# A hand-ordered attention and mixture-of-experts kernel: four scores for maxima, the routing steps and one projection change their places

## The chip, the core and the metric

One core of a Trainium2 chip runs the whole kernel. The metric is device time in microseconds (us). TensorE multiplies matrices into PSUM, VectorE, ScalarE and GpSimd work on vectors, SyncE issues transfers (DMA). Each engine runs its own list of instructions in order and waits at semaphores for the others.

## What is computed

Eight sequences of 256 tokens with 256 features, in fp32. `attn` is latent attention of 16 heads, each score of a content part (16) and a rotary part (64). `ffn` is multi-head attention (16 heads of 16) with its residual, then a mixture of 8 experts of which each token takes 2. Their product is gated:

```python
x = L0_attn_x
xn = _layernorm(x, axis=-1)
s = _L0_attn_ref(xn, ...)
g = _silu(_L0_ffn_ref(xn, ...))
x = x + s * g
```

with, inside,

```python
attn = jnp.where(causal[None, None], attn, -jnp.inf)
attn = jax.nn.softmax(attn, axis=-1)
...
top_logits, top_idx = jax.lax.top_k(logits, TOP_K)
probs = jax.nn.softmax(top_logits, axis=-1)
```

## The kernel before, in words

Weights are prepared first: products of weights are made once, and every operand of the projections is split into a high and a low part, so that one projection is three products (high by high, high by low, low by high). Then the eight batches b = 0 to 7 follow, one sequence each, and after them 23 blocks of rows for the experts and a last sum.

A batch is a pipeline of three stages, written out by hand for each engine (functions of the same names stand once in TensorE's part, once in ScalarE's, in VectorE's and in SyncE's):

- T1 (`stage_t1`): the latent attention of batch b. TensorE makes transposed scores, ScalarE the exponentials, GpSimd masks them, TensorE multiplies by the values. Beside each head stand scores of the multi-head attention, untransposed (`max2`), of which VectorE takes the causal row maxima (`maxima`, two instructions L1628 and L1631 for one head). `last_values` is the last group of T1's value products.
- P1 (`stage_p1`): the projections for batch b + 1, thirteen units in the order of `UNITS` (nq, nk: content; q0 to q3, k0 to k3: rotary, four heads each; mq, mk: multi-head; v: latent values). A unit is twelve matmuls. ScalarE copies nq and nk from PSUM to staging buffers (`keep_content`). The rotary units go through VectorE (`products`: one product with the cosines, L1571, one with the sines, L1572) and GpSimd (the sum), again into staging buffers, of which each is used for several units. SyncE then copies from the staging buffers to `qt` and `kt` inside SBUF (`place_content` L439, `place_rope` L446, `store_mha` L458). ScalarE rounds the landed heads (`rounded_q`, `rounded_k`), and TensorE makes the first four latent scores for maxima, head(0) and head(1) after mk, head(2) after q3, head(3) after k3. VectorE's maxima for them stand between the products 6 and 7.
- T2 (`stage_t2`): the multi-head attention of batch b with transposed scores, and beside it the untransposed latent scores of batch b + 1 for their maxima. After head 5 stands `project_v2`, the projection of the multi-head values of batch b + 1, twelve matmuls.

The row maxima go as one more row into the operands of the transposed scores. So, when all 16 multi-head maxima stand, TensorE transposes them (`max_t`, L728, with `rms_rows`, L814, ahead, which transposes a scale), ScalarE copies them (`max_t2`, line L1150 as every copy), and SyncE places them (`row2`, L419). SyncE's order inside its loop over the batches is

```python
row2(b)
stage_p1(b + 1)
```

and `row2` waits for `max_t2`; `stage_p1` begins with `place_content` of nq and nk, and goes on with q0, k0, q1, k1, q2, the multi-head stores, k2.

The routing of batch b - 1 lies in between: `top_two` on VectorE, `gate_exp` on ScalarE, `route_ranks` on TensorE (five small matmuls that count how many tokens of each expert come before), and VectorE's `positions` and `gates`, some dozen small instructions (L1718 to L1764), which before stand one or two at a time between the products.

Of the kernel before, what the change touches and what calls it, by code (L numbers as in the profile page):

```python
# [33 lines left out]
H, D, RD = 16, 16, 64  # L34
# [17 lines left out]
BANK = dict(nq=0, nk=1, q0=4, k0=5, q1=0, k1=1, q2=4, k2=5, mq=0, mk=1, q3=4, k3=5, v=0)  # L52
STAGED = dict(nq=1, nk=1, q0=2, k0=2, q1=2, k1=2, q2=2, k2=2, mqh=2, mkh=2, mql=2, mkl=2, q3=2, k3=2)
EARLY = 4
ST = 64
MROW2 = 3 * D
V1 = D
# [55 lines left out]
def build(nc, x, w_cols, w_dq, w_uqr, w_dkv, w_ukv, w_out, w_o, w_ln1, w_ln2, w_r, w_experts,  # L113
          cosines, sines, ident, mask, upper, route_c, slots, ones, out):
    ctx = ExitStack()
    with ctx:
# [260 lines left out]

        def ranks(r):

            return ps[3 if r + 2 <= last else 1]  # L380

        def v_heads(v, tt):

# [317 lines left out]
        def _(pe):  # L701
# [79 lines left out]
            def stage_p1(b, after):  # L781

                free = dict(q0=(ex1, 16 * b), k0=(ex1, 16 * b), q1=(nkd, 2 * b + 1), k1=(nkd, 2 * b + 2),
                            q2=(roped, 8 * b + 1), k2=(roped, 8 * b + 2), mq=(roped, 8 * b + 3),
                            mk=(roped, 8 * b + 4), q3=(roped, 8 * b + 5), k3=(roped, 8 * b + 6), v=(m2p, 2 * b + 1))
                for name in UNITS:
                    if name == "nq":
                        wait(pe, v2d, b)
                        wait(pe, xtld, b + 1)
                    elif name == "nk":  # L790
                        wait(pe, ohd, b - 1)
                    else:
                        wait(pe, *free[name])
                    if name == "k0" and b == 0:
                        pe.wait_ge(wdone, 1)
                        pe.wait_ge(wdonep, 1)
                    if name == "mq" and b == 0:
                        pe.wait_ge(wdone, N_DIRECT)
                    o = ps[BANK[name]]
                    if name == "v":  # L800
                        proj(o[:, 0:H * D], VC, H * D, 0)
                        i = proj(o[:, H * D:2 * H * D], VC, H * D, 1)
                    else:
                        features(o[:, 0:S], COLS[name])
                        i = features(o[:, S:2 * S], COLS[name] + P)
                    i.then_inc(p1d, 1)
                    after.get(name, lambda: None)()
# [26 lines left out]
            def max1(b):  # L834
                def head(h):
                    if h == 0:
                        wait(pe, mte2, b)
                        pe.wait_ge(rsd, b + 1)
                    elif h == 1:
                        wait(pe, pst, 6 * (b - 2) + 4)  # L840
                    if h % G == 0:
                        wait(pe, rrd, NG * b + h // G + 1)
                        wait(pe, rkd, NG * b + h // G + 1)
                    if h >= 2:
                        wait(pe, mx1, 16 * b + h - 1)
                    s = (NG * b + h // G) % RING
                    raw_scores(ps[2 + h % 2], qr[0:HW, s, h % G, :], kr[0:HW, s, h % G, :]).then_inc(m1d, 1)
                return head
# [53 lines left out]
            def stage_t1(b, after):  # L902
                def before_h0():
                    wait(pe, ex2, 16 * b)
                    wait(pe, md1, 16 * b + 16)
                    pe.wait_ge(s_one, 16)
                    wait(pe, v1d, b + 1)
                return heads(b, scores1, st1, ex1, exm1, pv1, ov1, v1, before_h0, lambda: wait(pe, x2d, b), max2(b),
                             {h: h + 2 for h in range(H - 2)}, lambda: None, after)

            def last_t2(after):
                def before_h0():
# [76 lines left out]
            def batch(b, first, more):  # L989
                to_tokens = None  # L990
                after1 = {}
                if not first:
                    to_tokens, back, project = close2(b - 1)
                    after1 = {1: back, 4: project, 11: lambda: route_transpose(b - 1),
                              14: lambda: route_logits(b - 1)}
                if more:
                    max2(b)(0)
                    max2(b)(1)
                    if not first:
                        to_tokens()  # L1000
                    after1[10] = lambda: transpose_x(b + 1)
                    last_values = stage_t1(b, after1)
                    to_tokens, back, project = close1(b)

                    def after_first():
                        last_values()
                        rms_rows(b + 1)
                        max_t(b, ps[2], negm2, mx2, mtr2)

                    def between():  # L1010
                        to_tokens()
                        if not first:
                            route_ranks(b - 1)
                    p1_with_m1(b + 1, {"nq": after_first, "k0": between, "k1": back})
                    stage_t2(b, max1(b + 1), {2: project, 5: lambda: project_v2(b + 1)})
                else:
                    max2(b)(0)
                    max2(b)(1)
                    to_tokens()
                    for h in range(H):  # L1020
                        if h % 2 == 0:
                            latent_head(h // 2)
                        if h >= 2:
                            max2(b)(h)
                        {4: back, 6: project}.get(h, lambda: None)()
                    latent_values(0)
                    max_t(b, ps[2], negm2, mx2, mtr2)
                    latent_values(1)
                    last_t2({1: lambda: route_transpose(b - 1), 4: lambda: route_logits(b - 1),
                             9: lambda: route_ranks(b - 1)})  # L1030
                    to_tokens, back, project = close2(b)
                    latent_head(8)
                    latent_head(9)
                    to_tokens()
                    latent_head(10)
                    latent_head(11)
                    back()
                    latent_head(12)
                    latent_head(13)
                    project()  # L1040
                    latent_head(14)
                    latent_head(15)
                    latent_values(2)
                    latent_values(3)
                    route_transpose(b)
                    route_logits(b)
                    to_tokens, back, project = close1(b)
                    to_tokens()
                    route_ranks(b)
                    back()  # L1050
                    project()
# [96 lines left out]
        def _(act):  # L1148
# [100 lines left out]
                i.then_inc(v1d, 1)  # L1249

            def stage_p1(b):
                if b > 0:
                    max_t2(b - 1)
                    rms_rows(b)
                keep_content(b, 0)
                keep_content(b, 1)
                if b >= 2:
                    gate_exp(b - 2)
                if b > 0:
                    keep_back(b - 1, fb1, of1, o1)  # L1260
                else:
                    rms_rows(b)
                rounded_q(b, 0)
                rounded_k(b, 0)
                mha_high(b, 0)
# [184 lines left out]
        def _(dve):  # L1450
# [144 lines left out]
            def max1(b, h):  # L1595
                maxima(b, h, h, negm1, m1d, mx1)
# [19 lines left out]
                    max1(b, h)  # L1616
                    after.get(h, lambda: None)()

            def stage_m2(b, after):
                wait(dve, mtr2, b)  # L1620
                for h in range(H):
                    maxima(b, h, (h % 2) * (H // 2) + h // 2, negm2, m2d, mx2)
                    after.get(h, lambda: None)()

            def maxima(b, h, col, negm, md, mx):
# [10 lines left out]
            def batch(b, first, more):  # L1636

                normalise, kept = ((lambda: None),) * 2 if first else close2(b - 1)
                if more:
                    after = {1: normalise, 3: lambda: normalised_two(b + 1), 6: kept, 13: lambda: x_low(b + 1)}  # L1640
                    if not first:
                        after[7] = lambda: stats_x2(b - 1)
                        after[10] = lambda: scale_x2(b - 1)
                else:
                    after = {1: normalise, 7: kept, 8: lambda: stats_x2(b - 1), 12: lambda: scale_x2(b - 1)}
                stage_m2(b, after)
                if not first:
                    top_two(b - 1)
                if more:
                    normalise, kept = close1(b)  # L1650
                    after = {1: normalise}
                    if not first:
                        in_expert, chosen, summed, marked, stepped = position_steps(b - 1)
                        plus_one, inverse, both = gate_steps(b - 1)
                        after = {1: lambda: (normalise(), in_expert()), 2: chosen, 3: lambda: (summed(), plus_one()),
                                 4: lambda: (marked(), stepped()), 5: lambda: (inverse(), both())}
                    stage_p1(b + 1, after)
                    stage_m1(b + 1, {7: kept})
                else:
                    positions(b - 1)  # L1660
# [314 lines left out]
```

## Time and profile before

| | |
|---|---|
| median of 3 runs | 809.52 us (809.34 to 810.34) |
| profiled execution | 808.98 us, span 807.2 us |
| mean granted TensorE clock | 0.953 |
| TensorE busy | 726.7 us, 90% |
| VectorE busy | 551.0 us, 68% |
| ScalarE busy | 429.0 us, 53% |
| GpSimd busy | 387.9 us, 48% |

The span runs from the first to the last instruction of the profiled execution; what lies around it is in the execution's time. PE is TensorE's matmuls, DVE VectorE, ACT ScalarE, POOL GpSimd, SPq the DMA queue of SyncE. A clock of 1.00 is the full one. In a timeline a row is a run of alike instructions: its start, its duration, engine, line, operation, output and inputs, their number, and in brackets the idle time before it and what ended that. Matmuls overlap, so the distance between two starts says more than a duration.

### The profile page before, as it was taken

Reading aid. Unit: us, or ns where it says so; the run is one execution under the profiler, and the core shown is the slowest. Engines: PE = TensorE matmul, PEld = TensorE weight load, DVE = VectorE, ACT = ScalarE, POOL = GpSimd, SP = SyncE. Lnnn points to the kernel's source line nnn. Section 1 sums busy time; section 2 is a strip of 40 time slices with the busy share of each in tenths; the row PEclk is TensorE's granted clock in tenths of the full one; section 3 lists DMA queues with packets and bytes.
Section 4 is the critical chain, followed back from the end, with each engine's and each line's share of the span. In section 5 each row is a group of like instructions: output and inputs, shape, how many; then the busy total and the mean of one; then the engine's idle time right before and its main releaser. Section 6 shows DMA issues by size and latency. Waiting matters only on the chain.

```text
span 807.2 us, 17047 instructions
## 1 busy us (share of the span) xinstructions
PE 726.7 (90%) x5968; PEld 651.0 (81%) x5968; DVE 551.0 (68%) x1925; ACT 429.0 (53%) x895; POOL 387.9 (48%) x489
## 2 busy tenths in 40 slices
PE   4869999999999999999999999894799999999970
PEld 3858978978988987887888887572699999999970
DVE  3876567687587586586586596425488888888844
ACT  2434364365365365355355445451487777887752
POOL 3642452354453453463563464253455666556640
PEclk9978999999999999999999999777799999999995
DMA  9492663573473474384284186431889999999736
GB/s 293 109 177 48 92 152 74 78 163 77 64 159 83 64 151 103 50 161 107 40 159 107 43 159 160 140 104 30 234 204 240 230 230 229 262 275 254 170 36 217
DMA packets 81416, 115.54 MB, mean 143 GB/s; under 512 B 17475, under 2 KB 57667, under 8 KB 81283
## 3 DMA queue, kind: packets, MB, share of 16 engines
q1 hardware_dynamic: 70612, 101.74, 53.0%
q0 software_dynamic: 9856, 12.13, 8.5%
q8 instruction: 47, 0.77, 0.4%
q10 hardware_dynamic: 864, 0.60, 0.3%
q14 instruction: 37, 0.30, 0.2%
HBM read 70.06 MB, written 23.46 MB: 116 GB/s over the span
## 4 chain that ended last, share of the span: by engine, by line
PE 69%; DVE 12%; DMA 6%; issue 4%; ACT 4%; SPq 4%; POOL 2%; DVEq 0%; POOLq 0%; ACTq 0%
PE ps L703 63%; DVE ex L1572 2%; ACT ex L1299 2%; DVE stg L1571 2%; DVE ps L1631 2%; DMA qt<-stg 2%; PE ps L739 2%; SPq L446 2%; PE ps L1097 1%; DVE ps L1628 1%; DMA ln<-in_w_ln 1%; POOL stg L607 1%; PE ps L748 1%; SPq L458 1%; SPq L402 1%
## 5 line engine op out<-in xcount | busy, mean ns | idle before, releaser
L647 POOL TENSOR_SCALAR_AFFINE_SELECT ex<-ex 128x256 f32<-128x256 f32 x256 | 102.9, 407 | 169.8 <-ACT ex L1299 157.7
L1299 ACT ACTIVATE ex<-ps 128x384 f32<-128x384 f32 x240 | 115.8, 490 | 122.3 <-PE ps L703 118.5
L703 PE MATMUL ps<-qt,kt 81*128 81x128 f32 (+2 forms) x768 | 165.5, 330 | 4.2 <-issue 2.0
L1628 DVE CUSTOM_DVE_ANT_0 ps<-ps,mask 128x128 f32<-128x128 f32 x256 | 78.1, 305 | 74.3 <-PE ps L703 72.6
L703 PEld LDWEIGHTS ps<-qt,kt 81*128 81x128 f32 (+1 forms) x768 | 111.1, 197 | 15.8 <-issue 7.9
L607 POOL TENSOR_TENSOR stg<-stg,ex 128x512 f32<-128x512 f32 x64 | 82.5, 1291 | 80.2 <-DVE ex L1572 78.3
L1631 DVE CUSTOM_DVE_ANT_0 ps<-ps,mask 128x256 f32<-128x256 f32 x256 | 119.1, 465 | 0.0
L690 POOL DMA_INDIRECT expert_rows<-yo,slot_of x46 | 75.4, 1639 | 82.6 <-ACT yo L1419 63.1
L1456 DVE TENSOR_TENSOR wel<-raw,weh 128x768 fp32r<-128x768 f32 x92 | 87.7, 956 | 18.3 <-ACT weh L1150 18.3
L703 PE MATMUL ps<-xth,wh 128*128 128x256 f32 x384 | 78.9, 286 | 2.0 <-issue 2.0
L1571 DVE TENSOR_TENSOR stg<-ps,cos_t 128x512 f32<-128x512 f32 x64 | 44.1, 689 | 52.8 <-PE ps L703 45.8
L703 PE MATMUL ps<-xeh,weh 128*128 128x256 f32 x368 | 78.0, 293 | 1.9 <-DVE xel L1854 1.9
L1150 ACT ACTIVATE weh<-raw 128x768 fp32r<-128x768 f32 x92 | 77.0, 837 | 0.0
L703 PE MATMUL ps<-xtl,wh 128*128 128x256 f32 x384 | 76.0, 279 | 0.0
L703 PE MATMUL ps<-xth,wl 128*128 128x256 f32 x384 | 76.0, 279 | 0.0
L703 PE MATMUL ps<-xel,weh 128*128 128x256 f32 x368 | 74.2, 283 | 0.0
L703 PE MATMUL ps<-xeh,wel 128*128 128x256 f32 x368 | 73.9, 282 | 0.0
L703 PE MATMUL ps<-kt,qt 128*128 128x128 f32 (+1 forms) x256 | 71.3, 368 | 1.5 <-DVE negm L1631 1.4
L703 PE MATMUL ps<-kr,qr 80*128 80x128 f32 (+1 forms) x256 | 56.4, 310 | 16.9 <-DVE negm L1631 7.9
L1402 ACT ACTIVATE sg<-ps 128x256 f32<-128x256 f32 x92 | 35.4, 385 | 50.6 <-PE ps L703 50.6
L703 PEld LDWEIGHTS ps<-xth,wh 128*128 128x128 f32 x384 | 58.6, 189 | 4.4 <-issue 4.2
L703 PEld LDWEIGHTS ps<-kr,qr 80*128 80x128 f32 x256 | 39.6, 195 | 27.5 <-DVE negm L1631 16.8
(157 smaller groups left out, 1682.1 us busy)
## 6 DMA issues: line engine op xcount, KB each, us to landing
raw<-in_w_experts SPq DMA_DIRECT2D x92, 384.0 KB, 4.5
qt<-stg SPq DMA_DIRECT2D x64, 128.0 KB, 4.0
kt<-stg SPq DMA_DIRECT2D x64, 128.0 KB, 3.8
multi_heads<-stg SPq DMA_DIRECT2D x64, 128.0 KB, 2.4
qt<-multi_heads SPq DMA_DIRECT2D x32, 192.0 KB, 3.6
kt<-multi_heads SPq DMA_DIRECT2D x32, 128.0 KB, 3.4
qt<-stg SPq DMA_DIRECT2D x8, 256.0 KB, 4.6
kt<-stg SPq DMA_DIRECT2D x8, 256.0 KB, 6.1
```

Of the source, the lines that this page charges most:

```text
L446: sp.dma_start(o, stg[:, s, t, :]).then_inc(sl[s], 16)
L607: nc.gpsimd.tensor_tensor(t, t, prb[:, n % 2, :, :], ALU.add).then_inc(tokd, 1)
L647: nc.gpsimd.affine_select(a, a, [[0, 2], [1, P]], ALU.is_ge, zero, 0, -1).then_inc(exm, 1)
L690: nc.gpsimd.indirect_dma_start(ys[:, :], bass.IndirectOffsetOnAxis(mt_b[:, blk, j, 1:2], 0), yo[:, blk % 2, j, :], None, compute_op=ALU.ad ...
L703: return nc.tensor.matmul(o, a, m, start=start, stop=stop, skip_group_check=True, **k)
L1150: return nc.scalar.activation(o, a, ACT.Copy)
L1299: nc.scalar.activation(ex[:, h % (2 * G), :], ps[4 + h % 2][:, P:4 * P], ACT.Exp, scale=scale).then_inc(ex_, 1)
L1402: nc.scalar.activation(sg[:, n % 2, :], ps[n % 3][:, 0:BS], ACT.Silu).then_inc(sgd, 1)
L1456: return nc.vector.tensor_tensor(o, a, b.bitcast(F32), ALU.subtract)
L1571: nc.vector.tensor_tensor(stg[:, s, :, :], a, cos_t[:, :].unsqueeze(1).broadcast_to([P, 2, S]), ALU.mult)
L1628: nc.vector.tensor_tensor_reduce(out=o[:, 0:P], in0=o[:, 0:P], in1=mask2[:, 1, :], scale=-1.0, scalar=-2.0 * BIG, op0=ALU.add, op1=ALU.min ...
L1631: nc.vector.tensor_tensor_reduce(out=o[:, S:2 * S], in0=o[:, S:2 * S], in1=mask2[:, :, :].rearrange("p a k -> p (a k)"), scale=-1.0, scala ...
```

## The change

Four things move, in the batches 0 to 6 (batch 0 has no routing yet); no instruction is added or taken away. SyncE's and GpSimd's lists stay as they are.

1. `BEHIND = 4`: T1 makes the untransposed multi-head scores ahead only up to head 11. Heads 12 and 13 are made behind unit nq, heads 14 and 15 behind nk. `last_values` comes after heads 12 and 13, `route_ranks` right after it (before: behind k0), into PSUM bank 5 instead of 3. `rms_rows` and `max_t` go from behind nq to behind q0.
2. ScalarE: `gate_exp` and the two content copies come ahead of `max_t2` and `rms_rows`.
3. VectorE: `positions` and `gates` stand in one piece between the maxima of heads 13 and 14; the products have no routing steps between them any more. The split of the transposed input (`x_low`) goes from after head 13 to after head 11.
4. T2: `project_v2` goes from after head 5 to after head 15, ahead of the last group of values.

```diff
+BEHIND = 4
...
-            return ps[3 if r + 2 <= last else 1]
+            return ps[5 if r + 2 <= last else 1]
...
+                        if name == "k0":
+                            wait(pe, pst, 6 * (b - 2) + 4)
...
-                    elif h == 1:
-                        wait(pe, pst, 6 * (b - 2) + 4)
...
-                             {h: h + 2 for h in range(H - 2)}, lambda: None, after)
+                             {h: h + 2 for h in range(H - BEHIND - 2)}, lambda: None, after)
...
-                    def after_first():
+                    head = max2(b)
+
+                    def after_nq():
+                        head(H - BEHIND)
+                        head(H - BEHIND + 1)
                         last_values()
+                        if not first:
+                            route_ranks(b - 1)
+
+                    def after_nk():
+                        head(H - BEHIND + 2)
+                        head(H - BEHIND + 3)
+
+                    def after_q0():
                         rms_rows(b + 1)
                         max_t(b, ps[2], negm2, mx2, mtr2)
-
-                    def between():
-                        to_tokens()
-                        if not first:
-                            route_ranks(b - 1)
-                    p1_with_m1(b + 1, {"nq": after_first, "k0": between, "k1": back})
-                    stage_t2(b, max1(b + 1), {2: project, 5: lambda: project_v2(b + 1)})
+                    p1_with_m1(b + 1, {"nq": after_nq, "nk": after_nk, "q0": after_q0, "k0": to_tokens, "k1": back})
+                    stage_t2(b, max1(b + 1), {2: project, H - 1: lambda: project_v2(b + 1)})
...
             def stage_p1(b):
+                if b >= 2:
+                    gate_exp(b - 2)
+                keep_content(b, 0)
+                keep_content(b, 1)
                 if b > 0:
                     max_t2(b - 1)
-                    rms_rows(b)
-                keep_content(b, 0)
-                keep_content(b, 1)
-                if b >= 2:
-                    gate_exp(b - 2)
+                rms_rows(b)
                 if b > 0:
                     keep_back(b - 1, fb1, of1, o1)
...
-                stage_m2(b, after)
+                stage_m2(b, range(H - BEHIND if more else H), after)
                 if not first:
                     top_two(b - 1)
                 if more:
                     normalise, kept = close1(b)
-                    after = {1: normalise}
+                    max2(b, H - BEHIND)
+                    max2(b, H - BEHIND + 1)
                     if not first:
...
-                        after = {1: lambda: (normalise(), in_expert()), 2: chosen, 3: lambda: (summed(), plus_one()),
-                                 4: lambda: (marked(), stepped()), 5: lambda: (inverse(), both())}
-                    stage_p1(b + 1, after)
+                        positions(b - 1)
+                        gates(b - 1)
+                    for h in range(H - BEHIND + 2, H):
+                        max2(b, h)
+                    stage_p1(b + 1, {1: normalise})
```

TensorE's list from the end of unit nq (`ps0`) to the start of nk (`ps1`), in the first batch that has routing; `ps7<-ex,v1` are last_values, `rms1` and `negm2` the transposes of rms_rows and max_t. Before:

```order
L703 MATMUL ps0<-xtl,wh 128x256 x2
L703 MATMUL ps7<-ex,v1 32x256 [waits mla_heads_kept,mla_exp_masked]
L703 MATMUL ps7<-ex,v1 32x256 x3
L703 MATMUL ps7<-ex,v1 32x128 x4
L814 MATMUL ps2<-idf,rms1 128x128 [waits mha_max,rms1_ready]
L814 MATMUL ps2<-idf,rms1 128x128
L728 MATMUL ps2<-idf,negm2 16x128 [waits mha_max]
L728 MATMUL ps2<-idf,negm2 16x128
L703 MATMUL ps1<-xth,wh 128x256 [waits experts_marked]
```

With the change (`kt2,qt2` are the untransposed multi-head scores, `ohb` the counts of ranks):

```order
L704 MATMUL ps0<-xtl,wh 128x256 x2
L704 MATMUL ps2<-kt2,qt2 128x128 [waits mha_max]
L704 MATMUL ps2<-kt2,qt2 128x256
L704 MATMUL ps3<-kt2,qt2 128x128 [waits mha_max]
L704 MATMUL ps3<-kt2,qt2 128x256
L704 MATMUL ps7<-ex,v1 32x256 [waits mla_heads_kept,mla_exp_masked]
L704 MATMUL ps7<-ex,v1 32x256 x3
L704 MATMUL ps7<-ex,v1 32x128 x4
L704 MATMUL ps5<-ohb,upb 128x8 [waits experts_marked]
L704 MATMUL ps5<-ohb,upb 128x8
L704 MATMUL ps5<-ohb,oneb 128x8 x3
L704 MATMUL ps1<-xth,wh 128x256 [waits experts_marked]
```

The two heads and the ranks have come between nq and nk; the transposes have left for a place two units later.

ScalarE's list at the start of P1, in the same batch; `ov` are T1's last value products, `mt` is max_t2, `rsb` rms_rows, `stg` the two content copies, `gexp` gate_exp. Before:

```order
L1150 ACTIVATE ov<-ps 128x256 [waits mla_pv] x2
L1150 ACTIVATE mt<-ps 16x256 [waits mla_max_row,mha_max_transposed]
L1150 ACTIVATE rsb<-ps 128x256 [waits mha_scaled,rms_rows_transposed]
L1150 ACTIVATE stg<-ps 128x512 [waits units_projected,staged_4_placed]
L1150 ACTIVATE stg<-ps 128x512 [waits units_projected,staged_5_placed]
L1326 ACTIVATE gexp<-gap 128x2 [waits logit_gap]
L1150 ACTIVATE otf<-ps 128x512 [waits mla_heads_back]
```

With the change:

```order
L1158 ACTIVATE ov<-ps 128x256 [waits mla_pv] x2
L1332 ACTIVATE gexp<-gap 128x2 [waits logit_gap]
L1158 ACTIVATE stg<-ps 128x512 [waits units_projected,staged_4_placed]
L1158 ACTIVATE stg<-ps 128x512 [waits units_projected,staged_5_placed]
L1158 ACTIVATE mt<-ps 16x256 [waits mla_max_row,mha_max_transposed]
L1158 ACTIVATE rsb<-ps 128x256 [waits mha_scaled,rms_rows_transposed]
L1158 ACTIVATE otf<-ps 128x512 [waits mla_heads_back]
```

The maxima's copy has gone from ahead of the content copies to behind them.

## Rows read from the trace of the kernel before

**Rows 1.** the page, part 4: chain that ended last, share by engine.

```profile
PE 69%; DVE 12%; DMA 6%; issue 4%; ACT 4%; SPq 4%; POOL 2%; DVEq 0%; POOLq 0%; ACTq 0%
```

**Rows 2.** TensorE's timeline, batch 5, T1 into P1: start us, us, operation [idle].

```profile
390.03 0.82 PE L703 MATMUL ps<-qt,kt 81*128 81x128 f32 x4
...
390.92 0.82 PE L703 MATMUL ps<-qt,kt 81*128 81x128 f32 x4
391.57 0.96 PE L703 MATMUL ps<-wr,s_b 128*128 128x8 f32 x8
...
394.00 0.51 PE L703 MATMUL ps<-xth,wh 128*128 128x256 f32 x2
...
395.61 0.86 PE L703 MATMUL ps<-ex,v 128*32 128x256 f32 x16
...
396.80 0.49 PE L703 MATMUL ps<-xth,wh 128*128 128x256 f32 x2
```

**Rows 3.** ScalarE's timeline, P1 of batch 6: copy of the transposed maxima.

```profile
397.08 0.37 ACT L1150 ACTIVATE mt<-ps 16x256 fp32r<-16x256 f32 x1 [0.17 <-PE ps L728]
```

**Rows 4.** timeline of SyncE's DMA queue, P1 of batch 6.

```profile
397.48 1.41 SPq L419 DMA_DIRECT2D qt<-mt  x2
399.01 0.62 SPq L439 DMA_DIRECT2D qt<-stg  x1
```

**Rows 5.** windows of P1: busy by engine, TensorE clock, DMA share, GB/s.

```profile
400.00:402.00 2.00, 2.00 (x20) 1.99 (x20) 1.89 (x3) 0.00 (x0) 0.63 (x1) 1.00 0.90 160
...
410.00:412.00 2.00, 1.49 (x13) 1.32 (x12) 1.97 (x4) 1.06 (x1) 0.90 (x1) 1.00 1.10 157
...
416.00:418.00 2.00, 2.00 (x19) 2.00 (x18) 2.00 (x7) 2.00 (x3) 1.78 (x2) 1.00 0.92 209
```

**Rows 6.** timeline of TensorE, end of P1 and start of T2.

```profile
411.70 0.70 PE L703 MATMUL ps<-kr,qr 80*128 80x128 f32 x4 [0.51 <-ACT kr L1150]
...
414.36 0.50 PE L703 MATMUL ps<-kr,qr 80*128 80x128 f32 x2 [0.55 <-DVE negm L1631]
...
418.44 0.50 PE L703 MATMUL ps<-qt,kt 128*128 128x256 f32 x2
```

**Rows 7.** VectorE's timeline, end of P1: a routing step, products of unit 6.

```profile
408.67 1.16 DVE L1747 TENSOR_SCALAR rc<-rc 128x8 f32<-128x8 f32 x1
...
415.30 0.69 DVE L1571 TENSOR_TENSOR stg<-ps,cos_t 128x512 f32<-128x512 f32 x1 [0.36 <-issue]
```

**Rows 8.** instructions of L446, 409.7:411.1: q2's two transfers, issue and landing.

```profile
L446 SPq DMA_DIRECT2D qt<-stg x2: 547/574/602, 409.8 to 410.4; - x2
...
DMA to landing us min/median/max: 3.8/4.1/4.4
```

**Rows 9.** TensorE's timeline: the first two matmuls of ranks (three follow).

```profile
401.97 0.20 PE L703 MATMUL ps<-ohb,upb 128*128 128x8 bf16 x2
```

**Rows 10.** timeline of TensorE, T2 of batch 4: project_v2 and the next scores.

```profile
361.26 0.40 PE L703 MATMUL ps<-wh,xth 128*128 128x256 f32 x2
...
362.68 0.40 PE L703 MATMUL ps<-qt,kt 128*128 128x256 f32 x2
```

**Rows 11.** timeline of VectorE, routing of batch 7 after the last T2.

```profile
551.00 0.17 DVE L1718 TENSOR_TENSOR pose<-ps,base 128x16 f32<-128x16 f32 x1 [0.38 <-PE ps L703]
...
552.69 0.15 DVE L1764 TENSOR_TENSOR meta<-gexp,gsum 128x2 f32<-128x2 f32 x1
```

**Rows 12.** VectorE's timeline, T2 of batch 4: two parts of latent maxima.

```profile
363.35 0.30 DVE L1628 CUSTOM_DVE_ANT_0 ps<-ps,mask 128x128 f32<-128x128 f32 x1 [0.65 <-PE ps L703]
...
363.94 0.33 DVE L1628 CUSTOM_DVE_ANT_0 ps<-ps,mask 128x128 f32<-128x128 f32 x1
```

**Rows 13.** windows of batch 7: busy by engine, TensorE clock, DMA share, GB/s.

```profile
509.40:516.10 6.70, 6.70 (x44) 4.29 (x46) 3.73 (x22) 3.20 (x6) 0.81 (x2) 0.50 0.12 41
```

**Rows 14.** TensorE's timeline: two waits, P1 of batch 4 and batch 7.

```profile
289.74 0.49 PE L703 MATMUL ps<-kr,qr 80*128 80x128 f32 x2 [1.30 <-DVE negm L1631]
...
508.63 0.50 PE L703 MATMUL ps<-kt,qt 128*128 128x128 f32 x2 [1.44 <-DVE negm L1631]
```

More of the change, by code:

```diff
@@ L1251, in stage_p1 @@
             def stage_p1(b):
+                if b >= 2:
+                    gate_exp(b - 2)
+                keep_content(b, 0)
+                keep_content(b, 1)
                 if b > 0:
                     max_t2(b - 1)
-                    rms_rows(b)
-                keep_content(b, 0)
-                keep_content(b, 1)
-                if b >= 2:
-                    gate_exp(b - 2)
+                rms_rows(b)
                 if b > 0:
                     keep_back(b - 1, fb1, of1, o1)
-                else:
-                    rms_rows(b)
                 rounded_q(b, 0)
@@ L1617, in stage_m1, with max2, stage_m2 @@
                     after.get(h, lambda: None)()
-            def stage_m2(b, after):
+            def max2(b, h):
+                maxima(b, h, (h % 2) * (H // 2) + h // 2, negm2, m2d, mx2)
+            def stage_m2(b, part, after):
                 wait(dve, mtr2, b)
-                for h in range(H):
-                    maxima(b, h, (h % 2) * (H // 2) + h // 2, negm2, m2d, mx2)
+                for h in part:
+                    max2(b, h)
                     after.get(h, lambda: None)()
@@ L1639, in batch @@
                 if more:
-                    after = {1: normalise, 3: lambda: normalised_two(b + 1), 6: kept, 13: lambda: x_low(b + 1)}
+                    after = {1: normalise, 3: lambda: normalised_two(b + 1), 6: kept, 11: lambda: x_low(b + 1)}
                     if not first:
@@ L1650, in batch @@
                     normalise, kept = close1(b)
-                    after = {1: normalise}
+                    max2(b, H - BEHIND)
+                    max2(b, H - BEHIND + 1)
                     if not first:
-                        in_expert, chosen, summed, marked, stepped = position_steps(b - 1)
-                        plus_one, inverse, both = gate_steps(b - 1)
-                        after = {1: lambda: (normalise(), in_expert()), 2: chosen, 3: lambda: (summed(), plus_one()),
-                                 4: lambda: (marked(), stepped()), 5: lambda: (inverse(), both())}
-                    stage_p1(b + 1, after)
+                        positions(b - 1)
+                        gates(b - 1)
+                    for h in range(H - BEHIND + 2, H):
+                        max2(b, h)
+                    stage_p1(b + 1, {1: normalise})
                     stage_m1(b + 1, {7: kept})
```

## The prediction

> **What bounds the kernel now.** I read the chain of waits first [rows 1]: TensorE holds 69% of it, VectorE 12%, DMA 6% and SyncE's queue (SPq) 4%. So most of a batch is TensorE work back to back, and the rest is a few places where something else ends last. The change touches the latent half's end (T1), the projections P1 of the next batch and the multi-head half (T2) of seven batches, so I took one steady batch, number 5, and followed P1 for batch 6 in the timelines of each engine, from 390 us to 419 us.
>
> TensorE's rows at the start of P1 [rows 2] show no idle time; the unit nq begins at 394.00, last_values at 395.61, and nk at 396.80. ScalarE copies the transposed multi-head maxima (mt) at 397.08 [rows 3], and SyncE sends that copy off (row2, L419) at 397.48 and only then the content rows (L439, 399.01) [rows 4]. From there a stream of copies inside SBUF runs: content, q0, k0, q1, k1, q2. In the windows the DMA share is 0.9 and more from 400 to 412, and the rate is about 160 GB/s at both ends [rows 5] (the first and the last of six such windows). At the end of the stream stand two waits. TensorE's first latent maximum, head(0), waits at 411.70 for ScalarE's rounded keys, which need k0's landing [rows 6]. And VectorE starts the products of unit 6 at 415.30, after 0.36 us idle [rows 7]: they write over the staging slot of q2, whose second transfer was issued at 410.42 and took 4.4 us [rows 8], so it landed at 414.8. T2's second head at 418.44 [rows 6] waits for VectorE's products of unit 7, which follow. So **the end of P1 is set by the landing of the stream**, though VectorE, which is nearly always busy there, shows little idle time.
>
> **The change part by part.** (a) Four heads leave T1. A head pair with its latent scores takes 0.89 us (390.03 to 390.92), the scores alone 0.65 (390.92 to 391.57) [rows 2]; so 0.24 us a head, 0.96 for four: nq begins 0.96 earlier. The work is not saved, it goes behind nq and nk, at 0.24 to 0.28 a head, about 1.05 for four.
>
> (b) The maxima's transposes (max_t) move behind q0. Before, from nq's start to the end of the transposes, 2.80 us pass: nq 1.61 with its switch, last_values, rms_rows and max_t together 1.19 [rows 2]. Now come nq 1.61, heads 12 and 13 0.55, ranks 0.15 (an estimate: five small matmuls that overlap, of which two take 0.20 [rows 9]), nk 1.42, heads 14 and 15 0.5, q0 1.42, and the same 1.19: 6.8 us. A unit's 1.42 is that of project_v2, which is twelve matmuls of the same kind (361.26 to 362.68) [rows 10]. Less the 0.96 of (a), max_t ends 6.8 - 2.8 - 0.96 = **3.0 us later**. VectorE must have the last maximum by then. Its one piece of positions and gates takes 1.84 us where it stands in one piece at the end (551.00 to 552.69 and 0.15) [rows 11], each maximum 0.59 (363.35 to 363.94) [rows 12]; two heads, the piece and two heads are 4.2 us, which about fits. The lower end of the shift is 3.0, the upper 3.4, or 5 if the small steps stretch as the one that took 1.16 us at 408.67 does [rows 7]; I take 3.0, the row of the uncontended piece being the nearest.
>
> (c) On ScalarE gate_exp and the two content copies now stand ahead of max_t2. That makes content ready earlier, but **nothing takes it**: SyncE's queue is in order and unchanged, and row2, which waits for max_t2, stands ahead of the content. What was issued at 397.48 goes at about 400.5, the content at 402.03 instead of 399.01 [rows 4]. Queued behind it are all of q0, k0, q1, k1, q2, the stores and the later loads.
>
> (d) Does the delay reach the end? The products of q0 to q2 are ready no later than before, so SyncE issues them back to back; but the stream has no pause from 400 to 412 [rows 5], so its landings move with its start. The lower end is 2.4 us (batches in which SyncE itself pauses a little), the upper 3.0; I take **2.7**. q2's landing, the products of unit 6 and 7 and T2's second head all come 2.7 later. head(0) finds its keys 3 us later: TensorE's wait there of 0.51 [rows 6] becomes about 3.5. A rule bears on this. "DMA: Bandwidth & Descriptors" of the Trainium skill, in Bandwidth, has a transfer of 1 MB at 341 GB/s; if the stream could run at that figure it would catch up, and this term would be 0. The windows, at under half of it, do not agree; they are the same stream, so they decide.
>
> (e) VectorE loses its routing steps among the products (two of them over 1 us when stretched, as the one of 408.67). Some 4 us come free, by those steps, but in front of a landing that comes later; worth nothing, except that the 0.55 wait of head(2) for a maximum (414.36) [rows 6] goes into the longer wait of head(0).
>
> (f) T2: project_v2 (1.42) leaves its place after head 5, where its matmuls starve VectorE of scores for 0.65 us (363.35) [rows 10, 12]; VectorE's maxima get that back. At the half's end the 1.42 stands in front of values(3), the last multi-head values. Between -0.2 (all hidden) and +1.4 (nothing hidden); I take **+0.4**, since TensorE is the engine that is full.
>
> (g) The clock. In the window 509.40 to 516.10 the granted clock is 0.50 [rows 13], the lower of the levels 1.2 and 2.4 GHz, and what stands before it is a TensorE wait of 1.44 us (508.63) [rows 14]. A wait of 1.30 (289.74) [rows 14] has no such stretch behind it. The new wait of 3.5 us is longer than both. A stretch of 6.7 us at half the clock costs at most half of it, 3.3 us of TensorE work; nothing if all of it lies where TensorE waits anyway. VectorE's chain to 418.44 still runs alongside, so I take **1.5**. "TensorE: Matmul & The Clock Gate" of the Trainium skill, in HAM oscillation, says that matmul bursts divided by waits for DMA are throttled and start cold each time; it speaks against the change. No row before shows such a wait in every batch, so by this rule the 1.5 stands in the sum, without it 0.
>
> **Sum.** Seven batches, each 2.7 + 0.4 + 1.5 = 4.6: 32.2 us. On the profiled execution's 808.98 that is 841.2; the median of the runs shown, 809.52, stands 0.5 above it, within the rounding: **841**.
>
> **The rivals.** A: the clock does not fall. Then 7 x 3.1 = 21.7 and 831, with 823 to 833 for the ends of (d) and (f). For it: the wait is one per batch with dense matmuls around it.
> B: the stream catches up in part, because in the new order SyncE no longer waits for products between issues and more transfers are in flight. With 0.5 to 2 us left per batch: 812 to 823.
> C, on the other side: the stream catches up wholly. Content to q2 would have to go at the 209 GB/s that the window 416 to 418 shows for stores [rows 5], against 160: some 12 us of stream would shrink by 3, just the delay. Then VectorE's freed time decides, and P1's two waits of 0.51 and 0.55 go [rows 6], with 0.3 to 0.4 given back by (f): 7 x -0.8 and **803**. It decides from a stream faster than about 205 GB/s. Against it: the windows in which the issues already ran ahead of the landings go at 157 and 160.
> D: half the clock for longer, over all of P1's tail and T2's first heads, two such stretches, 6.7 less what is hidden, so about 4.2 a batch in place of 1.5: 7 x 7.3 and 860.
> That the change does not do what it says is no rival: the instructions stand in the new order.
>
> **How the numbers follow.** The forecast case 0.45, A 0.25, B 0.10, C 0.08, D 0.08, no change 0.04. The forecast's own range is 832 to 852; the range from B's middle to D's, 817 to 860, leaves out the lower half of B, C, no change and half of D. Faster by over 0.2% is C, 0.08; within 0.2%, which is about what a measurement of this kernel can tell from no change, 0.04; slower 0.88.
>
> **What would show it.** Right: in a steady batch ScalarE's mt copy comes about 3 us later against T1's start, L439's first issue with it, q2 lands 2.4 to 3 later, TensorE waits some 3.5 us at its first kr,qr of P1, and windows of granted clock 0.5 follow. T1 is about 1 us shorter; VectorE has no wait of 0.65 after head 9. Wrong: content issued at the old distance, or landings spaced by less than 0.8 us for 128 KB, or a first kr,qr that waits under 1 us. A period per batch under the old one would show that VectorE's products, not the landing, had set the end.

## The result, and the profile after

| | before | changed |
|---|---|---|
| median | 809.43 us (807.96 to 810.34, 4 runs) | 832.22 us (830.41 to 835.56, 4 runs) |
| profiled execution | 808.98 us, span 807.2 us | 832.40 us, span 830.7 us |
| mean granted clock | 0.953 | 0.946 |
| ratio | | 1.0288 (95%: 1.0252 to 1.0324) |

The change makes the kernel 2.9% slower. The range held the time; the forecast of 841 was 9 us too high.

Two of the profiles further down (b_content_first, a_both_spread) are of executions that spent 48 to 51 us at half the clock ahead of batch 1's end, so of these two only distances inside the later batches are used; the medians below are of all executions, the ratios leave out those as slow as these two.

I went through batch 5 and P1 for batch 6 again, as ahead of the result. First the chain of the page's part 4, which answers to [rows 1]: DMA holds 11% of it instead of 6%, VectorE 7% instead of 12%.

```profile
PE 69%; DMA 11%; DVE 7%; SPq 4%; issue 3%; POOL 3%; ACT 2%; POOLq 0%; DVEq 0%; ACTq 0%
```

In part 5 (busy and mean ns, then idle time before the group and what ended most of it) the two groups that wait for the stream stand out: TensorE's untransposed latent scores, with 29.3 us of idle time, were at 16.9 us before, and 17.0 us of the idle time of VectorE's products now end with a landing.

```profile
L704 PE MATMUL ps<-kr,qr 80*128 80x128 f32 (+1 forms) x256 | 59.3, 322 | 29.3 <-ACT kr L1158 22.9
...
L1577 DVE TENSOR_TENSOR stg<-ps,cos_t 128x512 f32<-128x512 f32 x64 | 44.2, 691 | 31.5 <-DMA qt<-stg 17.0
```

TensorE's timeline from nq to the transposes answers to [rows 2]. From 412.71 (nq) past heads 12 and 13 (414.23), last_values and heads 14 and 15 (417.20) to the next unit at 419.53 it is 6.82 us, against 6.8 in the working.

```profile
412.71 0.50 PE L704 MATMUL ps<-xth,wh 128*128 128x256 f32 x2
...
414.23 0.62 PE L704 MATMUL ps<-kt,qt 128*128 128x128 f32 x4
414.77 0.86 PE L704 MATMUL ps<-ex,v 128*32 128x256 f32 x16
...
417.20 0.62 PE L704 MATMUL ps<-kt,qt 128*128 128x128 f32 x4
...
419.16 0.40 PE L817 MATMUL ps<-idf,rms 128*128 128x128 f32 x2
...
419.53 0.48 PE L704 MATMUL ps<-xth,wh 128*128 128x256 f32 x2
```

ScalarE's copy of the maxima [rows 3] and SyncE's queue [rows 4] follow:

```profile
417.46 0.60 ACT L1158 ACTIVATE stg<-ps 128x512 f32<-128x512 f32 x1 [0.80 <-PE ps L704]
419.81 0.37 ACT L1158 ACTIVATE mt<-ps 16x256 fp32r<-16x256 f32 x1 [1.75 <-PE ps L729]
```

```profile
420.21 1.42 SPq L420 DMA_DIRECT2D qt<-mt  x2
421.75 0.62 SPq L440 DMA_DIRECT2D qt<-stg  x1
```

The second content copy was done at 418.06 (its row on ScalarE), and the content still waited until row2 had gone at 420.21: 421.75. From T1's start it is 28.81 us to the content, before 25.53: 3.28 later, and 3.2 to 3.3 in each of the later batches. The stream then takes as long as before. q2's rows answer to [rows 8]; its issue now runs ahead by more (7.2 us to landing instead of 4.4), its landing does not.

```profile
L447 SPq DMA_DIRECT2D qt<-stg x2: 547/575/603, 429.8 to 430.4; - x2
...
DMA to landing us min/median/max: 6.9/7.0/7.2
```

VectorE's products of unit 6 [rows 7], the last product of unit 7 (440.00) and TensorE's head(0) and T2's second head [rows 6]:

```profile
437.61 0.69 DVE L1577 TENSOR_TENSOR stg<-ps,cos_t 128x512 f32<-128x512 f32 x1 [1.88 <-DMA qt<-stg]
...
440.00 0.68 DVE L1578 TENSOR_TENSOR ex<-ps,sin_t 128x512 f32<-128x512 f32 x1
```

```profile
433.73 0.75 PE L704 MATMUL ps<-kr,qr 80*128 80x128 f32 x4 [2.82 <-ACT kr L1158]
...
440.97 0.40 PE L704 MATMUL ps<-qt,kt 128*128 128x256 f32 x2
```

The wait at head(0) is 2.82 us (2.3 to 3.8 over the seven batches); VectorE stands 1.88 us for the landing. In all seven batches unit 6 starts 0.02 us after q2's second transfer landed (its landing time in the trace); before, it starts 0.02 to 1.2 us after it. (In the first batch, which has no routing steps, it waited for the landing before the change too, 1.72 us.)

Distances in us, from the starts and landings in the two traces, batches 2 to 7 by the batch whose projections are made (T1 is the first latent score of the batch, T2 the second head's first score):

| from, to | before | changed |
|---|---|---|
| T1 to the content's issue | 25.53 | 28.81 |
| content to q2's landing | 15.1 to 16.3 | 15.3 to 16.7 |
| T1 to the end of the products of unit 7 | 44.92 | 47.2 to 48.6, mean 47.8 |
| T1 to T2's second head | 44.97 | 47.3 to 49.0, mean 48.0 |
| T2's second head to the next T1 | 17.37 | 17.65 to 17.95, in one batch 19.60 |
| period | 62.35 | 66.1 |

Six periods are 22.5 us more, the first batch 3.2; that is 25.7 at the last batch's T1. From there to the first expert matmul the traces show 72.9 us before and 69.4 after, of which 37.9 and 29.3 at half the clock; that stretch differs by 4.7 us between two profiles of one kernel too (a_both and a_both_again below: 74.3 and 69.6), so what the changed kernel has back by the end (2.2 us with the blocks behind) is not the change's.

The granted clock fell in six of the seven batches, for 3.4 us each time. Five of the falls begin 0.1 to 1.4 us behind the wait of head(0), in P1's tail; the sixth lies in T2. The columns are those of [rows 5]:

```profile
431.00:434.20 3.20, 0.47 (x4) 0.50 (x5) 0.69 (x1) 2.56 (x4) 0.51 (x1) 1.00 1.17 154
434.25:437.60 3.35, 3.35 (x18) 3.35 (x17) 1.37 (x8) 2.39 (x3) 2.56 (x2) 0.50 1.17 156
```

```profile
308.00:311.30 3.30, 3.30 (x10) 2.76 (x10) 1.32 (x8) 0.49 (x1) 1.04 (x3) 0.50 0.41 119
```

### The profile page after: what moved, and what is told of

It reads as the page before. It is cut to its first block, busy times and chain, and to the rows that moved or that the text cites. A ratio compares the mean times of both kernels' runs of the same rounds, so it can differ in the third digit from the quotient of the medians.

```text
span 830.7 us, 17053 instructions
## 1 busy us (share of the span) xinstructions
PE 737.7 (89%) x5968; PEld 657.4 (79%) x5968; DVE 540.8 (65%) x1925; ACT 428.8 (52%) x895; POOL 387.3 (47%) x489
## 4 chain that ended last, share of the span: by engine, by line
PE 69%; DMA 11%; DVE 7%; SPq 4%; issue 3%; POOL 3%; ACT 2%; POOLq 0%; DVEq 0%; ACTq 0%
PE ps L704 63%; DMA qt<-stg 4%; DMA kt<-stg 3%; SPq L447 2%; DMA expert_rows<-yo,slot_of 1%; PE ps L1105 1%; PE ps L740 1%; DMA ln<-in_w_ln 1%; DVE ps L1640 1%; POOL stg L608 1%; DVE ex L1578 1%; DVE stg L1577 1%; ACT ex L1305 1%; SPq L459 1%; DVE ps L1637 1%
## 5 line engine op out<-in xcount | busy, mean ns | idle before, releaser
L704 PE MATMUL ps<-qt,kt 81*128 81x128 f32 (+2 forms) x768 | 162.7, 327 | 5.7 <-DVE ex L1578 2.3
L704 PE MATMUL ps<-kr,qr 80*128 80x128 f32 (+1 forms) x256 | 59.3, 322 | 29.3 <-ACT kr L1158 22.9
L704 PE MATMUL ps<-xth,wh 128*128 128x256 f32 x384 | 82.4, 297 | 2.0 <-issue 2.0
L704 PE MATMUL ps<-xth,wl 128*128 128x256 f32 x384 | 78.5, 287 | 0.0
L704 PE MATMUL ps<-xtl,wh 128*128 128x256 f32 x384 | 78.4, 286 | 0.0
L704 PE MATMUL ps<-xel,weh 128*128 128x256 f32 x368 | 74.3, 284 | 0.0
L704 PEld LDWEIGHTS ps<-xth,wh 128*128 128x128 f32 x384 | 61.4, 198 | 4.5 <-issue 4.3
L704 PE MATMUL ps<-kt,qt 128*128 128x128 f32 (+1 forms) x256 | 63.2, 344 | 1.8 <-DVE negm L1640 1.8
```

What stands on the lines that cost most here:

```text
L704: return nc.tensor.matmul(o, a, m, start=start, stop=stop, skip_group_check=True, **k)
```

## The experiments

Three theories were to be told apart. **Landing**: the content leaves late because row2 stands ahead of it in SyncE's queue, and the stream's end sets the end of P1. **Order of work**: the heads and ranks among the units, or VectorE's one piece, cost by themselves. **Clock**: the fall behind the long wait is a good part of it.

**a_content_first** undoes the queue's delay alone:

```diff
                 row2(b)
                 stage_p1(b + 1)
...
+                wait(sp, st1, 16 * (b + 1))
+                place_content(b + 1, 0)
+                place_content(b + 1, 1)
                 row2(b)
                 stage_p1(b + 1)
```

(`stage_p1` itself leaves the two out for b above 0.)

> The changed kernel, but SyncE sends the content rows (nq, nk) ahead of row2. Landing theory (the end of P1 is set by the stream of copies, which starts late because row2 stands ahead of the content in SyncE's queue): the content leaves about 5 us earlier than in the changed kernel, TensorE's wait of 2.3 to 3.8 us at head(0) goes, a batch gets 2.4 to 3 us shorter: 832.2 - 7 x 2.7 = 813 us (808 to 818). Rival, order of TensorE's work (the four heads and the ranks among the units cost by themselves, the wait only hides it): the wait goes and as much time comes back in P1, 828 to 834 us.

Measured: 809.96 us, 0.9987 of the kernel before (0.9966 to 1.0008), where the changed kernel is at 1.0288. The whole loss is gone. SyncE's queue now has the content ahead of the maxima, 23.80 us after T1 (28.81 in the changed kernel):

```profile
399.01 0.59 SPq L440 DMA_DIRECT2D qt<-stg  x1
400.36 0.56 SPq L440 DMA_DIRECT2D kt<-stg  x1
402.49 1.45 SPq L420 DMA_DIRECT2D qt<-mt  x2
```

and TensorE comes to head(0) without a wait:

```profile
413.03 0.62 PE L708 MATMUL ps<-kr,qr 80*128 80x128 f32 x4
```

The order of work falls: it is all still there. T1 to T2's second head takes 44.4 us on the mean of batches 2 to 7, 0.58 less than before; T2 takes 17.93 (19.34 in one batch, in which the clock falls) where it took 17.37, so the two about cancel.

**b_delay** does the opposite: the kernel before, with nothing moved on TensorE but the transposes, to behind q0.

```diff
                     def after_first():
                         last_values()
+
+                    def after_q0():
                         rms_rows(b + 1)
                         max_t(b, ps[2], negm2, mx2, mtr2)
```

ScalarE's two content copies stand ahead of max_t2 there too.

> The kernel before, with only rms_rows and max_t moved from behind nq to behind q0 (and ScalarE's content copies ahead of max_t2); heads 12 to 15, the routing steps and project_v2 stay where they were. Landing theory: max_t ends two units later, 2 x 1.42 = 2.8 us, row2 and the content in SyncE's queue with it, and the stream's end too: 809.4 + 7 x 2.6 = 827.6 us (824 to 831). Rival, order of TensorE's and VectorE's work (the moved heads and the one piece of routing are what costs): 808 to 812 us.

Measured: 832.59 us, 1.0296 (1.0276 to 1.0316): **by the median the delay alone gives the whole loss**, a little more than expected. Its seven executions lie between 825.85 and 837.44 us, and the profiled one is the fastest: there the delay gives 17 of the 23 us. Its last T1 starts at 516.05, 7.8 us ahead of the changed kernel's; of the rest of the change, project_v2 (7 x 0.56, below), 0.42 us a batch of longer delay and one fall of the clock in T2 (1.65) are 8.5. Why the other six executions took 4 to 12 us longer no trace shows; their mean granted clock is lower, 0.928 to 0.938 against 0.942. From nq at 341.93 to the unit behind the transposes it is 5.66 us instead of 2.80, the content leaves 28.39 us after T1, 2.86 later than before, and VectorE stands 1.49 us for q2's landing.

```profile
341.93 0.51 PE L703 MATMUL ps<-xth,wh 128*128 128x256 f32 x2
...
347.45 0.38 PE L728 MATMUL ps<-idf,negm 128*16 128x128 f32 x2
347.59 0.48 PE L703 MATMUL ps<-xth,wh 128*128 128x256 f32 x2
```

```profile
348.27 1.43 SPq L419 DMA_DIRECT2D qt<-mt  x2
349.81 0.63 SPq L439 DMA_DIRECT2D qt<-stg  x1
```

```profile
366.53 0.69 DVE L1571 TENSOR_TENSOR stg<-ps,cos_t 128x512 f32<-128x512 f32 x1 [1.49 <-DMA qt<-stg]
```

**b_content_first**: the kernel before with the content copies ahead on ScalarE and the content ahead of row2 in SyncE's queue, the same edits as above.

> The kernel before, with only the content copies ahead of max_t2 on ScalarE and the content rows ahead of row2 in SyncE's queue. Landing theory: the stream starts 0.5 to 1.4 us earlier, but VectorE's chain, with the routing steps among the products, then sets the end of P1 (its wait for the landing was 0.36): 809.4 - 7 x 0.4 = 806.6 us (804 to 809). Rival, the landing alone set the end: 809.4 - 7 x 1.2 = 801 us.

Measured: 808.51 us, 0.9995 (0.9976 to 1.0013): no change. The content leaves 1.54 us earlier (23.99 after T1), q2 lands 0.2 to 1.6 us earlier in five of the six later batches, and the period is 62.34 against 62.35; the products of unit 6 start 41.8 us after T1 in both, 0.4 to 1.7 us after the landing. So in the six later batches of the kernel before it was VectorE's chain that set the end of P1, and the landing lay 0 to 1.2 us under it.

**a_project_early** puts project_v2 back behind head 5, in the changed kernel:

```diff
-                    stage_t2(b, max1(b + 1), {2: project, H - 1: lambda: project_v2(b + 1)})
+                    stage_t2(b, max1(b + 1), {2: project, 5: lambda: project_v2(b + 1)})
```

> The changed kernel with project_v2 back behind head 5 of T2. Theory: its place at the half's end costs the 0.3 to 0.55 us by which T2 grew in the traces (17.37 before, 17.65 to 17.95 after): 832.2 - 7 x 0.4 = 829.4 us (828 to 831). Rival: T2 grew for another reason (it starts with fewer scores ahead, since VectorE's products come late), then 832 us, no change. Second rival: the late place is a gain hidden by the rest, then 833 us or more.

Measured: 831.91 us, 1.0266 (1.0246 to 1.0286); the expected gain is not resolved by the times. In its trace T2 takes 17.1 to 17.5 us, and the last T1 starts at 520.20 instead of 523.86; the stretch from there to the first expert matmul takes 2.9 us more (72.3 against 69.4), so little of it reaches the time.

**a_both** has this edit and a_content_first's:

> Both edits: content rows ahead of row2 and project_v2 behind head 5. Landing theory: the sum of both, 813 - 3 = 810 us (805 to 815), no better than the kernel before by more than 0.5%. Rival, VectorE's freed time is worth something once the landing is early: under 804 us.

Measured: 806.81 us, 0.9955 (0.9933 to 0.9977), inside the landing theory's range. **a_both_again** repeats it beside the next kernel:

> a_both once more, beside the other three on one chip: 0.993 to 0.998 of the kernel before, 805 to 808 us. T2 without a fall of the clock takes 17.1 to 17.7 us from its second head to the next T1, with one about 1.7 more; the number of such falls differs from run to run.

Measured: 803.96 us, 0.9947 (0.9925 to 0.9969). The time is under the expected 805 to 808, the ratio inside the expected range. This version is some 0.5% faster than the kernel before, with both intervals under 1. With the content early, the edit is worth what its T2 shows: 17.37 us in a_both_again against 17.93 in a_content_first, 0.56 a batch, where the clock stays up. In one batch T2 has a fall of the clock (232.1 to 235.5) and takes 19.04, 1.7 more.

**a_both_spread** tells what VectorE's part is worth there. It is a_both with the routing steps among the products again:

```diff
                     if not first:
-                        positions(b - 1)
-                        gates(b - 1)
...
+                        in_expert()
+                        chosen()
+                        after = {1: normalise, 2: summed, 3: plus_one,
+                                 4: lambda: (marked(), stepped()), 5: lambda: (inverse(), both())}
                     for h in range(H - BEHIND + 2, H):
                         max2(b, h)
-                    stage_p1(b + 1, {1: normalise})
+                    stage_p1(b + 1, after)
```

> The kernel a_both (change, content rows first, project_v2 behind head 5), but the routing steps behind the first two stand between VectorE's products again, as before the change. If VectorE's freed time is worth something once the landing is early, P1 gets longer by up to 1 us per batch: a_both + 4 us (2 to 7). Rival, TensorE sets the end of P1 there: as a_both within 1 us.

Measured: 809.08 us, 1.0013 (0.9992 to 1.0035), 0.66% over a_both_again on the same chip, 5.3 us. Six of the seven batches have routing, so that is 0.88 a batch, and T1 to T2's second head takes 45.22 on the mean of these six against 44.34. Among the products two steps are stretched as at [rows 7], and unit 6 starts behind VectorE's own chain, at 430.85:

```profile
424.22 1.14 DVE L1766 TENSOR_SCALAR rc<-rc 128x8 f32<-128x8 f32 x1
...
426.66 1.29 DVE L1462 COPY meta<-gsum 128x2 f32<-128x2 f32 x1
...
430.85 0.69 DVE L1581 TENSOR_TENSOR stg<-ps,cos_t 128x512 f32<-128x512 f32 x1 [0.36 <-issue]
```

Both stretched steps end 0.02 to 0.03 us after a sum of GpSimd that was under way when they began:

```profile
424.05 1.29 POOL L612 TENSOR_TENSOR stg<-stg,ex 128x512 f32<-128x512 f32 x1 [0.55 <-DVE ex L1582]
...
426.63 1.29 POOL L612 TENSOR_TENSOR stg<-stg,ex 128x512 f32<-128x512 f32 x1 [1.30 <-DVE ex L1582]
```

In the one piece of the changed kernel the same two steps take 0.17 each (VectorE, columns as above), and in a_both_again unit 6 waits for q2's landing again, 0.02 us ahead of its start in every batch:

```profile
417.02 0.17 DVE L1757 TENSOR_SCALAR rc<-rc 128x8 f32<-128x8 f32 x1
...
417.50 0.17 DVE L1458 COPY meta<-gsum 128x2 f32<-128x2 f32 x1
```

```profile
413.57 0.69 DVE L1581 TENSOR_TENSOR stg<-ps,cos_t 128x512 f32<-128x512 f32 x1 [0.86 <-DMA qt<-stg]
```

**a_filler** was to take the fall of the clock out of P1: 18 matmuls ahead of the wait of head(0) in the changed kernel.

```diff
                         pe.wait_ge(rsd, b + 1)
+                        for _ in range(3):
+                            features(ps[2][:, 0:S], COLS["mk"])
```

> The changed kernel with 18 more matmuls (about 2.1 us) in front of TensorE's wait for the first keys, into a bank that head(0) overwrites, so that TensorE hardly idles there; nothing else moves. Landing theory with a cheap clock: the wait shrinks from 2.3 to about 0.2 us, the granted clock stays at 1.00 in P1, and the time stays at 830 us (828 to 833), since at half the clock TensorE still comes before the landing. Clock theory (the prediction's 1.5 us per batch): 832 - 10 = 822 us.

Measured: 841.24 us, 1.0385 (1.036 to 1.041), slower than the changed kernel by about 9 us; neither theory had that. The wait shrank (0.20 at 170.96, batch 2; 0.2 to 0.3 in five batches, but 1.53 and 1.44 in two), and no fall lies in P1's tail any more, but in five of the seven batches the clock now falls just behind T2's second head, after TensorE's waits for the products of units 6 and 7:

```profile
170.96 0.70 PE L704 MATMUL ps<-kr,qr 80*128 80x128 f32 x4 [0.20 <-ACT kr L1160]
...
177.30 0.47 PE L704 MATMUL ps<-qt,kt 128*128 128x256 f32 x2 [0.92 <-DVE ex L1580]
...
179.00 0.50 PE L704 MATMUL ps<-qt,kt 128*128 128x256 f32 x2 [0.58 <-DVE ex L1580]
```

```profile
177.30:180.40 3.10, 2.20 (x11) 1.52 (x12) 3.10 (x17) 2.11 (x5) 2.59 (x3) 1.00 0.38 111
180.50:183.90 3.40, 3.40 (x11) 2.77 (x10) 1.14 (x7) 0.40 (x1) 0.88 (x3) 0.50 0.39 111
```

In those five, T2 takes 19.5 to 19.6 us, in the two others 17.9: 1.5 to 1.7 each time. The price of a fall in T2 is thus measured five times here, once in the changed kernel (19.60 against 17.95) and once in a_content_first (19.34 against 17.93, 1.4). And P1 without falls is no shorter: T1 to T2's second head takes 47.9 us on the mean of batches 2 to 7, where the changed kernel takes 48.0.

## Why the prediction was right

(a) and (b), the delay of max_t, 3.0: measured 3.28. The working from nq on was exact (6.82 against 6.8). What was off is the gain in T1: nq begins 19.77 us after T1 instead of 20.51, 0.74 earlier, not 0.96.

(c) The content behind row2 in SyncE's queue: shown from both sides, by a_content_first (take the order away: no loss) and b_delay (only the delay: all the loss by the median, 17 of 23 us in the traced execution).

(d) The stream, 2.7: the end of the products of unit 7 comes 2.3 to 3.7 us later, 2.9 on the mean. The stream did not catch up, though SyncE issued q0 to k1 1.5 to 3 us sooner behind the content than before: rival B, with more transfers in flight, and rival C, on the other side, did not come. From q0 to q2 the transfers of 128 KB land 0.87 us apart on the mean of batch 6 before, and 0.86 after, whether the queue is ahead by 4 us or by 7. The 341 GB/s that "DMA: Bandwidth & Descriptors" of the Trainium skill has in Bandwidth is for 1 MB from HBM into SBUF; in these copies inside SBUF it has no counterpart (154 and 156 GB/s in the windows from 431 to 437.6). One reading of the prediction was wrong here: the 0.36 us ahead of unit 6 [rows 7] was not a wait for q2's landing. It stands in the same place in a_both_spread (430.85, above), and in b_content_first an earlier landing gave nothing. The end of P1 was VectorE's, with the landing at most 1.2 us under it and 0.40 on the mean of the six later batches. A delay of 3.28 less this slack is 2.88, just the 2.89 measured; the prediction's ground for taking 2.7 of 3.0, pauses of SyncE, was another, so the nearness is in part luck.

(e) VectorE's freed time "worth nothing" held for the change as it is. It was hidden: with the landing early it is worth 0.88 us a batch (a_both_again against a_both_spread), which is what makes a_both faster than before. Rival C's idea was right about the worth and wrong about how one gets there.

(f) project_v2, +0.4: measured 0.56 at the same clock (T2 of a_content_first against a_both_again), within its bounds.

(g) **The step that was mis-sized is the clock, 1.5 us a batch.** The clock does fall behind the wait, as forecast, in five batches of seven, and rival A's ground for 831 (no fall) is wrong although its number is nearest. (Its range, 823 to 833, is not what the ends of (d) and (f) give: 7 x 2.2 to 7 x 4.4 make 825 to 840.) But in P1's tail TensorE has time: at half the clock it still comes to the products before VectorE gets the landing. T2's second head comes 0.06 us after the products of unit 7 in the two batches without a fall in P1 and in two of the five with one, and 0.3 to 0.5 after them in the other three; T2 is 0.3 shorter behind these. So a fall there cost next to nothing (0 to 0.2), and only the one in T2 its 1.65: 0.2 to 0.3 a batch instead of 1.5, or some 8.5 us of the 9 by which the forecast was too high. The other terms, 0.36 a batch above the working, and the shorter stretch at the end about cancel. The rule in "TensorE: Matmul & The Clock Gate" of the Trainium skill, HAM oscillation, that bursts divided by waits for DMA start cold, agrees with the trace in five batches (granted 0.50 from 434.25 on), and not in the two in which no fall follows in P1 on waits of 2.37 and 2.27 us. And not every cold start is paid for.

## What to carry to other kernels

An early transfer that stands behind a late one in an in-order queue is as late as that one: when a producer is moved back, look at what its consumer's queue holds behind it, and move the queue's order along with it. Read the slack of the second-latest releaser too: before the change the landing was hidden by 1.2 us at most, so 3 us of delay came through almost whole. A gain on an engine that another one covers (VectorE's one piece of routing) shows only after the cover is gone, so a change of four parts is to be tried part by part.

## What was not expected of the hardware

A fall of the granted clock costs by its place: 1.4 to 1.7 us for 3.4 us at half the clock in T2, 0 to 0.2 in P1's tail. And filling a wait with matmuls did not rid the kernel of falls: they came later, behind short waits of 0.92, 0.17 and 0.58 us at T2's start, where they cost, and the kernel became 1% slower. These waits alone do not decide it: a_filler has the last of them, 0.58 or 0.59, in all seven batches and falls in five, and a_both_again has 0.42 to 0.58 in six and a fall in one. What else does is open. In the kernel before, T2 starts without such waits in the six later batches [rows 6] (the first has 0.59) and kept the full clock in all seven.

VectorE's small routing steps took 1.14 and 1.29 us among the products and 0.17 each in one piece, the same two instructions. In the traces of the kernel before and of a_both_spread each of the twelve such steps among the products lies beside a sum of GpSimd of about 1.3 us and ends 0.02 to 0.03 us after it; in the one piece no sum is under way, and none of the steps is stretched. No run moved GpSimd's sums away, so this is read from the traces and not tried.
